# Expert-weight splitting cut in two on GpSimd, and the hidden transposes set between the second and third group of the down product, in an attention and top-2 MoE layer

## The reference

```python
x = x + _layernorm(_L0_attn_ref(_layernorm(x), Wq, bq, Wk, bk, Wv, bv, Wo, bo))   # 16 heads of 16, RoPE on q and k
x = x + _layernorm(_L0_ffn_ref(_layernorm(x), centroid, Wg, bg, W1, b1, W2, b2))
...
def _moe_forward(x, centroid, Wg, bg, W1, b1, W2, b2):       # E = 8 experts, K = 2, H = 684
    d2 = |xs|^2 + |centroid|^2 - 2 xs @ centroid.T
    w, sel = jax.lax.top_k(sqrt(d2), K);  w = softmax(w)
    for e in range(E):
        h = silu(xs @ Wg[e] + bg[e]) * (xs @ W1[e] + b1[e])
        out = out + we[:, e:e + 1] * (h @ W2[e] + b2[e])
```

## Time and profile before

| | us |
|---|---|
| median of 3 runs (lowest, highest) | 1670.2 (1669.54, 1672.49) |
| the profiled execution, own time | 1676.76 |
| its span in the trace | 1674.0 |
| PE busy | 1444.0 (86%) |
| DVE busy | 1112.5 (66%) |
| ACT busy | 968.4 (58%) |
| POOL busy | 548.2 (33%) |
| attention, 143 to 901: PE busy of 758 | 653.3 |
| MoE loop, 1053 to 1630: PE busy of 577 | 568.0 |

### The profile page before, as it was taken

How to read it: one execution, slowest core, us unless ns; L and a number is a source line. 1 busy time by engine, 2 the same in 40 slices (tenths; PEclk the granted TensorE clock), 3 DMA queues, 4 the chain that set the end, 5 groups by cost and what they waited for, 6 DMA issues and landing times.

```text
span 1674.0 us, 31840 instructions
## 1 busy us (share of the span) xinstructions
PE 1444.0 (86%) x10413; PEld 893.7 (53%) x10414; DVE 1112.5 (66%) x1890; ACT 968.4 (58%) x1755; POOL 548.2 (33%) x464
## 2 busy tenths in 40 slices
PE   7899969696969889696999862799999999999980
PEld 5454424232323333242334431788888988988970
DVE  7999968696969878696832659355545555555544
ACT  4525867585858767585887542354445444544544
POOL 5740041203040211303131323344444444444424
PEclk9999988797989989897999985899999999999985
DMA  6975444365754635374123952544444444444556
GB/s 201 280 191 91 109 109 137 66 185 131 186 76 152 93 101 88 60 161 75 65 68 83 230 199 125 167 128 118 115 115 125 126 118 119 131 118 116 154 149 204
DMA packets 181487, 220.38 MB, mean 132 GB/s; under 512 B 57583, under 2 KB 152748, under 8 KB 178837
## 3 DMA queue, kind: packets, MB, share of 16 engines
q1 hardware_dynamic: 165493, 200.52, 45.1%
q0 software_dynamic: 15904, 18.66, 6.4%
HBM read 146.64 MB, written 72.48 MB: 131 GB/s over the span
## 4 chain that ended last, share of the span: by engine, by line
PE 50%; DVE 25%; issue 13%; POOL 7%; DMA 2%; SPq 2%; ACT 1%; DVEq 0%; POOLq 0%; ACTq 0%
DVE mx L1084 17%; PE psum L1862 13%; PE psum L1844 5%; PE psum L1842 5%; PE psum L1843 5%; PE psum L1697 4%; PE psum L1670 4%; PE psum L1852 3%; POOL split_raw L884 3%; PE psum L1684 2%; DVE psum L1077 2%; PE psum L1630 2%; PE psum L1644 1%; POOL w_lo L890 1%; PE psum L1771 1%
## 5 line engine op out<-in xcount | busy, mean ns | idle before, releaser
L1466 ACT ACTIVATE work<-psum 128x512 f32<-128x512 f32 x1024 | 544.3, 600 | 200.8 <-PE psum L1684 177.4
L1084 DVE TENSOR_REDUCE mx<-psum 128x1 f32<-128x1024 f32 (+1 forms) x512 | 547.3, 1096 | 47.3 <-PE psum L1670 35.1
L1670 PE MATMUL psum<-stack 48*128 48x512 f32 x1024 | 388.2, 462 | 105.9 <-DVE mx L1084 96.4
L1684 PE MATMUL psum<-stack 50*128 50x512 f32 x1024 | 386.9, 464 | 0.0
L1670 PEld LDWEIGHTS psum<-stack 48*128 48x128 f32 x1024 | 167.4, 193 | 355.0 <-DVE mx L1084 251.9
L1697 PE MATMUL psum<-work,values 128*32 128x384 f32 x4080 | 316.4, 407 | 0.2
L1842 PE MATMUL psum<-w_hi,x_hi 128*128 x568 | 188.4, 332 | 1.0 <-DVE x_lo L1302 1.0
L1844 PE MATMUL psum<-w_hi,x_lo 128*128 x568 | 182.4, 321 | 0.0
L1317 DVE TENSOR_TENSOR h_lo<-psum,h_hi 128x768 fp32r<-128x768 f32 x71 | 68.0, 958 | 171.1 <-ACT h_hi L1551 171.1
L1843 PE MATMUL psum<-w_lo,x_hi 128*128 x568 | 181.6, 320 | 0.0
L1684 PEld LDWEIGHTS psum<-stack 50*128 50x128 f32 x1024 | 166.9, 193 | 24.3 <-ACT work L1466 18.8
(11 more groups left out here) (201 smaller groups left out, 2088.7 us busy)
## 6 DMA issues: line engine op xcount, KB each, us to landing
stack<-qk_scr SPq DMA_DIRECT2D x192, 128.0 KB, 6.2
work<-in_w SPq DMA_DIRECT2D x36, 640.0 KB
small<-in_w SPq DMA_DIRECT2D x35, 640.0 KB
qk_scr<-weights SPq DMA_DIRECT2D x16, 1024.0 KB, 4.7
split_raw<-in_w SPq DMA_DIRECT2D x8, 1368.0 KB
wh_d<-w_hi SPq DMA_DIRECT2D x6, 1368.0 KB, 5.7
w_hi<-wh_d SPq DMA_DIRECT2D x6, 1368.0 KB, 12.0
ot_scr<-weights SPq DMA_DIRECT2D x16, 512.0 KB, 3.2
```

Of the source, the lines that this page charges most:

```text
L1084: dve.tensor_reduce(mx[:, r, a, t:t + 1], scored, AX, ALU.max, negate=True).then_inc(s_max, 1)
L1466: act.activation(pt[u % 4][:, j, :], bank((c + HG * u + n) % 3), ACT.Exp, scale=SC).then_inc(s_exp, 1)
L1670: ins = pe.matmul(bank(4 + 2 * a + half), qs[t3][at:at + QROWS, r, P * t:P * (t + 1)], ks[t3][at:at + QROWS, r, 512 * half:512 * (half + 1 ...
L1684: pe.matmul(bank((t3 + HG * u + n) % 3), ks[t3][at:at + MROWS, r, P * st:P * (st + 1)], qs[t3][at:at + MROWS, r, 512 * half:512 * (half + ...
```

## The change

It has three parts. In attention `split_weights` becomes `high_weights` (subtractions and rounding copies) and `low_weights` (the rests); the first moves ahead of `copy_values`, the second one group later, between the two calls of `split_max`. In the MoE loop the down product always uses 128 rows (the sixth block is padded), and PE runs `turn_hidden(t)` between its second and third group; around that, ACT rounds W2 of tile t at the end of tile t instead of in the middle of t + 1, gated by a new semaphore `s_dh` that PE raises behind the second group; DVE makes `w2_lo` first in its tile. And `y_row` gets a second buffer, so that the scatter of a tile runs one tile later, ahead of the gathers; it newly waits for `s_mt`, which PE raises behind `turn_rows`.

```diff
-        y_row = c.take([C])
+        y_row = [c.take([C]) for _ in range(2)]
...
-            def split_weights(n):
-
-                p, at, raw, high = n % 2, split_in[n], split_raw[split_in[n]], w_hi[:, high_in[n], :, :]
+            def high_weights(n):
+
+                p, raw, high = n % 2, split_raw[split_in[n]], w_hi[:, high_in[n], :, :]
...
+            def low_weights(n):
+
+                at, raw, high = split_in[n], split_raw[split_in[n]], w_hi[:, high_in[n], :, :]
                 for k in range(KC):
                     pool.wait_ge(s_split, split_steps(n, 1) + k + 1)
                     pool.tensor_tensor(w_lo[:, at, k, :], raw[:, k, :], high[:, k, :].bitcast(F32), ALU.subtract).then_inc(s_split, 1)
...
-                if not (isinstance(g, int) and g + 1 >= NG):
-                    for r in range(PAIRS):
+                for r in range(PAIRS):
+                    if not (isinstance(g, int) and g + 1 >= NG):
                         split_max(g + 1, r)
+                    for n, at in enumerate(SPLIT_AT):
+                        if r == 0 and g == at + 2:
+                            low_weights(n)
+                        if r == 1 and g == at + 1:
+                            high_weights(n)
                 if not (isinstance(g, int) and g + 2 >= NG):
                     copy_values(i, c + 2)
-                for n, at in enumerate(SPLIT_AT):
-                    if g == at + 1:
-                        split_weights(n)
...
-            def scatter(t):
+            def scatter(t, p):
+                if not isinstance(t, int) or t + 4 <= NS:
+                    pool.wait_ge(s_mt, t + 4)
                 pool.wait_ge(s_is, t + 1)
                 pool.wait_ge(s_yr, t + 1)
...
+            def tile(t, p):
+
+                if not isinstance(t, int) or t >= 2:
+                    scatter(t - 2, p)
+                if not isinstance(t, int) or t + 3 < NS:
+                    gather(t + 3, 1 - p)
+                if not isinstance(t, int) or t + 2 < NS:
+                    gather_weight(t + 2)
...
             def low_w2(t, p):
                 dve.wait_ge(s_w2h, t + 1)
+                after(dve, s_yp, t)
...
                 if not first:
-                    low_hidden(t - 1)
+                    low_w2(t - 1, 1 - p)
                 multiply(t, 0)
                 if not first:
-                    low_w2(t - 1, 1 - p)
+                    low_hidden(t - 1)
+                if not isinstance(t, int) or t >= 2:
+                    aim_scatter(t - 2)
                 multiply(t, 1)
...
-                after(act, s_yp, t)
+                after(act, s_dh, t)
...
                 gate(t, 0)
-                if not first:
-                    high_w2(t - 1, 1 - p)
                 gate(t, 1)
                 if not isinstance(t, int) or t + 1 < NS:
                     high_x(t + 1)
+                high_w2(t, p)
                 if not first:
-                    save_y(t - 1)
+                    save_y(t - 1, 1 - p)
...
-            def down(t):
-                after(pe, s_yr, t)
+            def down(t, parts):
+                if 0 in parts:
+                    after(pe, s_yr, t)
...
                     for k in range(KH):
-                        rows = P if k < KH - 1 else LAST + 1
-                        last = pe.matmul(bank(7)[:, 0:C], h[0:rows, k, :], w[0:rows, k, :],
-                                         start=n + k == 0, stop=(n, k) == (2, KH - 1))
-                last.then_inc(s_yp, 1)
+                        last = pe.matmul(bank(7)[:, 0:C], h[:, k, :], w[:, k, :], start=n + k == 0, stop=(n, k) == (2, KH - 1))
+                    if n > 0:
+                        last.then_inc((s_dh, s_yp)[n - 1], 1)
...
                 if not (isinstance(t, int) and t == 0):
-                    down(t - 1)
+                    down(t - 1, (0, 1))
                 turn_hidden(t)
+                if not (isinstance(t, int) and t == 0):
+                    down(t - 1, (2,))
```

More of the change, by code:

```diff
@@ L420, in build @@
         s_hl = sem("hidden_t_low_ready")
+        s_dh = sem("expert_out_of_high_weights")
         s_yp = sem("expert_out_ready")
@@ L974, in _ @@
             pool.wait_ge(s_wd, 32)
-            for t in range(2):
-                gather(t, t)
-                gather_weight(t)
-            gather(2, 0)
-            gather(3, 1)
-            gather_weight(2)
-            for t in range(1, 2):
-                gather(t + 3, (t + 3) % 2)
-                gather_weight(t + 2)
-                scatter(t - 1)
+            def tile(t, p):
[5 more added lines that the diff above has]
+                    gather_weight(t + 2)
+            gather(0, 0)
+            gather(1, 1)
+            gather_weight(0)
+            gather(2, 0)
+            gather_weight(1)
+            for t in range(2):
+                tile(t, t)
             with pool.Fori(1, (NS - 3) // 2) as i:
                 for p in range(2):
-                    t = 2 * i + p
-                    gather(t + 3, 1 - p)
-                    gather_weight(t + 2)
-                    scatter(t - 1)
-            for t in range(NS - 3, NS + 1):
-                if t + 2 < NS:
-                    gather_weight(t + 2)
-                scatter(t - 1)
+                    tile(2 * i + p, p)
+            for t in range(NS - 3, NS + 2):
+                tile(t, t % 2)
             pool.wait_ge(s_x2r, 16 * (NT // 4))
@@ L1363, in _ @@
             aim_weight(1)
-            for t in range(2):
-                tile(t, t)
-            with dve.Fori(1, (NS - 3) // 2) as i:
+            for t in range(4):
+                tile(t, t % 2)
+            with dve.Fori(2, (NS - 3) // 2) as i:
                 for p in range(2):
@@ L1370, in _ @@
                 tile(t, t % 2)
+            low_w2(NS - 1, (NS - 1) % 2)
             low_hidden(NS - 1)
-            low_w2(NS - 1, (NS - 1) % 2)
+            aim_scatter(NS - 2)
             aim_scatter(NS - 1)
@@ L1554, in high_w2, with save_y @@
                 act.wait_ge(s_w2[p], 48 * ((t - p) // 2 + 1) if isinstance(t, int) else 24 * (t - p) + 48)
-                after(act, s_yp, t)
+                after(act, s_dh, t)
                 act.activation(w2_hi[:, :, :].rearrange("p k n -> p (k n)"), w2_raw[p].rearrange("p k n -> p (k n)"),
                                ACT.Copy).then_inc(s_w2h, 1)
-            def save_y(t):
+            def save_y(t, p):
                 act.wait_ge(s_yp, t + 1)
-                after(act, s_ys, 16 * t)
+                after(act, s_ys, 16 * (t - 1))
                 act.wait_ge(s_wk, t + 1)
-                act.activation(y_row, bank(7)[:, 0:C], ACT.Copy, scale=w_all[:, bass.ds(t, 1)]).then_inc(s_yr, 1)
+                act.activation(y_row[p], bank(7)[:, 0:C], ACT.Copy, scale=w_all[:, bass.ds(t, 1)]).then_inc(s_yr, 1)
             def tile(t, p):
@@ L1575, in tile @@
                     high_x(t + 1)
+                high_w2(t, p)
                 if not first:
-                    save_y(t - 1)
+                    save_y(t - 1, 1 - p)
             high_x(0)
-            for t in range(2):
-                tile(t, t)
-            with act.Fori(1, (NS - 1) // 2) as i:
+            for t in range(4):
+                tile(t, t % 2)
+            with act.Fori(2, (NS - 1) // 2) as i:
                 for p in range(2):
@@ L1891, in _ @@
             tile(NS - 1, (NS - 1) % 2)
-            down(NS - 1)
+            down(NS - 1, (0, 1, 2))
 def layout(inputs):
```

8 lines of the change are left out of this document (4 added, 4 removed).

## The result

The changed kernel takes **1598.4 us** (median of 4 runs, 1593.3 to 1614.6) against 1669.9 of before (4 runs): a ratio of 0.959, 95% interval 0.952 to 0.966. Forecast were 1474 us, in a range from 1462 to 1518. The change gains 71.5 us where 196 were expected. The two profiled executions, spans 1674.0 and 1599.1, differ by 74.9 us.

The account below looks back on a forecast made before the run. It took DVE's waits for POOL's cut maxima to bound attention and PE (199.13 of 200 us busy) the MoE loop. 1676.8 - 111.1 - 80.5 - 5 = 1480.2 us; that execution stood 6.6 above the median, hence 1474, range 1462 to 1518.

Parts of the forecast that it names:

- The attention part: Attention: the split's high and low parts fit into POOL's idle time, removing the whole stall; -111 us over seven groups.
- rival 3: Attention's gain comes in part: bias row 5 us later gives 1495 us, half the stall 1530; 11 in 100.
- The row part: MoE loop's down product: without short blocks 1.15 us less a tile, -80.5 us over 70 periods, period 6.83 us.
- Rival 2: MoE loop's down product: the short block isn't the cost, so the loop stays as it is; 1554 us, 5 in 100.
- What the other edits cost: MoE loop: moved scatter, gathers, W2's rounding and rest cost nothing, with 0.6 to 1.1 us of slack left.
- The prediction's last sentence: MoE loop: a wait on PE, as a tile's chain through four engines lost its slack, would above all prove it wrong.
- The chain of durations: MoE loop: from s_dh over rounding, w_lo, multiplication and h_lo to PE's second group, 0.6 to 1.1 us of slack.
- Rival 1: MoE loop: a starting scatter delays PE's messages by 1.8 us, closing a 7.25 us ring; 1503 us, 28 in 100.
- The ring of 1503 us: MoE loop: scatter, delayed s_dh, rounding, w_lo, multiplication, h_lo, cast, next scatter; 7.25 us a period, 29 us given back.
- The loop's end: Behind the last gate product: short blocks gone, transposes and W2's rounding earlier; -5 us together.

Follow-up runs that it names:

- e1_attention: The kernel before with only POOL's attention part changed (high part ahead of copy_values, low part between the halves' maxima): 1572.5 us, ratio 0.942.
- e8_bias_early: e3_weight_first with SP's issue of an expert's bias row moved ahead of the wait for the second half's maxima: 1493.1 us.
- e3_weight_first: The changed kernel with POOL's gather of slot weights ahead of its gather of rows, DVE's two casts swapped to match: 1498.8 us, ratio 0.895.
- e5_weight_first_45: e3_weight_first with 45 rows again in the sixth block of the down groups: 1568.8 us.
- e4_45_rows: The changed kernel with 45 rows again in the sixth block of the down groups: 1612.6 us.
- e6_short_w2_load: The changed kernel with only one of the five full blocks of W2 loaded for a tile: 1490.2 us.
- e7_w2_rest_one_input: The changed kernel with DVE making W2's rest from one operand (W2 times zero) instead of a subtraction of two: 1552.2 us.
- e10_rows_plain_store: The kernel before with 128 rows in the sixth down block and the scatter replaced by a plain DMA to spare rows: 1591.6 us.
- e9_weight_first_no_turn_wait: e3_weight_first with the scatter's wait for turn_rows left out: 1495.9 us.

## Why the prediction was wrong

**The attention part: right, a little large.** Forecast -111, measured -105.7 over the same groups. The whole part is confirmed alone by e1_attention. What is missing lies mostly in the groups with the bias row. The prediction gave it 1.8 us from issue to landing. Seven of the eight in the changed kernel took 1.7 to 1.9 us, but one of them shows otherwise; SP had issued two stores of an expert's parts just ahead of it:

```profile
257.46 0.43 SPq L607 DMA_DIRECT2D wl_d<-w_lo  x1
257.94 0.82 SPq L600 DMA_DIRECT2D split_raw<-in_b  x1
```
```profile
265.58 6.20 POOL L885 TENSOR_TENSOR split_raw<-split_raw 128x1368 f32<-128x1368 f32 x2 [11.89 <-DMA split_raw<-in_b]
```

7.6 us, rival 3 in small: that group took 44.2 us, 4.5 more than one without a split. With the row issued early (e8_bias_early) it takes 39.7, and the 13 groups 523.5 us, within 0.3 us of the forecast's 634.3 - 111.1. But e3_weight_first, whose attention is that of the changed kernel, has 524.3, so that the late row costs 1 to 5 us, by how much the next group gives back.

**The row part: the price right, its place wrong.** 1.15 us a tile was forecast; e5_weight_first_45 against e3_weight_first gives 1.10, and the period with PE as the bound is 6.77 beside the 6.83 forecast. Rival 2 is refuted by that. The price is paid at three places in the trace: 0.21 us between starts ahead of the short block, 0.31 behind it, and 0.22 at the pair after that, where 0.12 is usual: 0.38 us a turn. The rule that the prediction cites from the Trainium skill, "TensorE: Matmul & The Clock Gate", Why this matters for your kernels, speaks of a single matmul, which no run here shows; it doesn't carry over to this stream, where the change to 45 rows and back costs 0.37 us (1.10 for three). But in the changed kernel PE isn't the bound, and e4_45_rows shows the rows to be worth 2 us of loop at most.

**The step that failed** is "What the other edits cost", in its sentence "gather is for three tiles ahead, some 13 us in advance, and that cover is wide". It is true of the rows. The loop took 588.5 us, where the forecast comes to 477.9: 110.6 of the 124 us that the forecast missed by. The slot weights are gathered by the same engine behind the rows, for one tile ahead only, into a single buffer, and `keep_weight` has to free that buffer before the next gather. In the order of before the copy stood behind h_lo, both multiplications and w_lo, at the end of a tile of 7.9 us; the ring took some 5.6 us of it and hid: copy and casts 0.3, until the row gather 0.7, until the weights' gather 1.3, landing 3.3. (With 0.35, 0.7, 2.3 and 4.8 it is 8.2 in the changed kernel, and the next copy 0.1 behind it.)

Three things came together after the change. The casts stand right ahead of w_lo, which stretches the row gather from 0.99 to 2.2 us; w_lo's end then releases W2's load just ahead of the slot weights' gather, which lands after 4.8 instead of 3.3 us (medians; the load is issued 0.1 us ahead of the gather, where before it was 1.95 us, and in e3_weight_first, with a landing of 2.4 us, 3.7); and w_lo now stands behind keep_weight as the first thing of the next tile. The ring seems to feed its own delay, which no run tests by itself: a late copy makes a late w_lo, which makes a late load, beside which the next slot weights land late. e3_weight_first, e6_short_w2_load and e7_w2_rest_one_input each take a link out or shorten it, and the loop falls by 110, 112 and 52 us. The prediction's last sentence named a wait on PE in the loop as what would prove it wrong. That is where it failed, by a chain that it had not worked out: none of its rivals has the slot weights.

**The chain of durations was right.** The slack of 0.6 to 1.1 us that the prediction worked out for the chain from s_dh to h_lo exists, and is 1.2 us (median of e3_weight_first, from h_lo's end to the start of the second group; the chain's own sum, 2.0 + 0.51 + 0.96, is 3.5 and not 3.4): where the slot weight is out of the way, PE doesn't wait at all. The reorder of the change does its work there. It takes the loop from 524.0 (rows alone, old order) to 478.7, and the forecast had 558.4 - 80.5 = 477.9. What does it is not the slack alone: the scatter has left gate_up with the new order, and the old order without the scatter's delay has 482.8 (e10_rows_plain_store).

**Rival 1 named a true mechanism at the wrong place.** e10_rows_plain_store shows that a scatter delays what gate_up tells the others; e9_weight_first_no_turn_wait shows that s_dh, 1.1 us behind a scatter's start, is not delayed. The ring of 1503 us never formed.

**The loop's end:** forecast -5, measured -1.3. The last scatter waits for its addresses, whose buffer is free only when the scatter before has landed:

```profile
1550.70 1.56 POOL L964 DMA_INDIRECT y_d<-values,at_y  x1 [5.06 <-issue]
1555.45 1.56 POOL L964 DMA_INDIRECT y_d<-values,at_y  x1 [3.19 <-DVE at_y L1340]
```

The sum as measured on the profiled executions: attention -105.7, what lies between it and the loop +2.0, loop +30.1, end -1.3: -74.9.

## What to carry to other kernels

When a chain of work is moved, follow every buffer that one of the moved instructions frees, not only the largest: here 512 bytes of slot weights in one buffer set the pace of a loop that loads 0.7 MB of W2 (684 x 256 x 4 bytes) a tile. A load's cover is its distance to its reader minus the time until it may be issued at all; where the reader's copy also releases the next load, compute the length of that ring with the durations under load, and order the issues on an engine by how soon their data is needed. A saving on the bounding engine is worth its price only down to the next ring: measure each part alone, since the rows gave 34 us in one order, 2 in another, and 73 in the third.

## What was not expected of the hardware

An indirect gather issued by POOL takes 0.96 to 0.99 us alone and up to 2.4 us when a long DVE instruction over SBUF operands began ahead of it; one of 1.76 us adds 1.2 us on average, one of 0.96 us 0.4 us, with two operands or one, and the gather ends some 0.86 us behind it. One that reads PSUM (h_lo, 0.96 us) adds nothing. An indirect scatter of 1.62 us delays what PE's gate products tell DVE and ACT until 1.8 us after its own start, a plain store of the same rows (0.60 us) until 0.6 us, and a gather doesn't. Why the message behind the down product isn't delayed in the same way, and why none is in the unrolled tail, stays open. And three turns from blocks of 128 rows to one of 45 and back cost 1.10 us in a stream of matmuls that otherwise follow each other by 0.12 us, so that padding to 128 rows, with more work, is faster.
